# Loading one-hots of places from a table, splitting the queries into three bf16 parts, and gathering 110 of 220 pairs of tiles without an add

## The chip, the cores and the metric

The kernel runs on one core of a Trainium2 chip. The time is the device time of the whole kernel in microseconds (us). Before the change three runs gave 3959.79, 3951.86 and 3950.71 us, a median of 3951.86 us.

## The reference, cut to what matters

Four graph layers run one after the other on 3,125 nodes with 256 channels and 53,125 edges, sorted by destination. Each adds its result to the node rows and normalizes them. The fourth, which the change is mostly about, is a transformer convolution that runs twice (here called its two halves):

```python
q = (x @ Wq + bq).reshape(n, H, C)          # H = 4 heads, C = 64 channels
k = (x @ Wk + bk).reshape(n, H, C)
v = (x @ Wv + bv).reshape(n, H, C)
e = (edge_attr @ We + be).reshape(-1, H, C)
k_j = k[src] + e
q_i = q[dst]
alpha = jnp.einsum('ehc,ehc->eh', q_i, k_j) / jnp.sqrt(C)
...                                          # softmax of alpha over the edges of each dst
msg = (v[src] + e) * alpha[..., None]
out = jax.ops.segment_sum(msg, dst, num_segments=n)
```

The first layer and the third are attention layers too, with one score for a node in place of a row of queries: an edge needs the score of its destination.

## The kernel before

**Tiles.** The edges are cut into 440 tiles of 128 (`ET`), each of which has its destinations in one block of 128 nodes (25 blocks, `NT`). Two tiles are a pair (220 pairs), eight tiles a group (`HB`, 55 groups), sixteen tiles a batch of the softmax (`NB`). The program is a row of phases with a barrier between them: `start_up`, `aggregate0`, `finish0`, `aggregate1`, `finish1`, `aggregate2`, `finish2`, `attend(1)`, `between`, `attend(2)`, `last_rows`. `finish2` and `between` make queries, keys and values of the fourth layer from the node rows (class `Projection`), and `attend` goes over the edges.

**One-hots of places.** TensorE fetches the destination's row for each edge by a matmul with a one-hot matrix `ohT` (places in the block by edges). `lo_tab` in DRAM holds each edge's place as bf16. For each group the SyncE queue (SP) spreads 1,024 places over 128 partitions (`lo_b`, 256 KB), and VectorE (DVE) compares them with the partition's number: `places(g)` in `aggregate2` (line 1348) and `attend` (line 1761), `one_hots(g)` in `aggregate0` (line 532). In `attend` the one-hots and the queries `H` are f32; in the aggregates one-hots and scores are bf16, the scores as three bf16 parts that are summed.

**attend, a step for each pair p.** Each engine has its order written out, and semaphores join them:

- GpSimd (POOL) issues an indirect DMA for each tile that gathers 128 rows of `kv_tab` (keys, values, and four columns for weights: 516 f32) by source. In 55 of the 220 pairs (`plain(p)`, p % 8 in (4, 6)) the rows are written to the buffer `kv` (line 1737). In the others the DMA adds them to what stands there (`compute_op=ALU.add`, line 1741), which are the edge terms.
- TensorE (PE) makes the edge terms of a pair (`edge_terms`, line 1922), f32, six steps ahead for a pair with an add and one step ahead for a plain pair, then the queries of pair p + 1 (`queries`, line 1933), then the scatter of pair p - 11 (`scatter`, line 1951).
- ScalarE (ACT) copies the edge terms from PSUM to `kv` twice, as key and as value part, for pairs with an add (`fill(p + 5)`, lines 1862 and 1863), makes the one-hots of the scatter, and weighs two of four heads.
- DVE, for a plain pair, adds the edge terms to keys and values (`add_edge_terms`, lines 1769 and 1771). For each pair it multiplies keys by queries (`times_q`, line 1781), sums by channels (line 1787), adds two windows of sums to `acc` (line 1817), and takes its share of the softmax. Once in four pairs it makes a group's one-hots of places (line 1761) and weighs two heads (line 1795).
- SP loads for each group the edge attributes (`aT`, 512 KB, line 1748) and the places (line 1751), each when a ring of three has room.

**finish2 and between.** For each of 25 blocks t, PE turns the rows (`turn`), ACT copies them (`take_turned`, line 1521), PE multiplies them by the weights (`products`, line 1513), and DVE takes the four results with their biases (`take`, lines 1538 to 1544), the queries into `H`. The rows are turned two blocks ahead.

## Time and profile before

| | before |
|---|---|
| median of three runs | 3951.86 us |
| profiled execution, its own time | 3946.54 us |
| its span, first to last instruction | 3944.8 us |
| busy: PE, DVE, POOL, ACT | 2936.7, 2698.3, 2560.9, 1981.6 us |
| mean granted TensorE clock | 0.869 of full speed |
| stretch of aggregate2 / finish2 / attend(1) | 587 / 139 / 803 us |
| stretch of between / attend(2) | 112 / 801 us |

Busy times are unions of an engine's instructions, which overlap a little. PE's are modelled at their ends. The stretches are cut at phase ends read from the timeline, and their sum of five is 2442 us of the span.

### The profile page before, as it was taken

To read this page: it belongs to the slowest core of one execution; us is meant where nothing else is said; L and a number is where in the kernel's file an instruction comes from. 1 tells how busy PE (TensorE), PEld (TensorE's weight loads), DVE (VectorE), ACT (ScalarE), POOL (GpSimd) and SP (SyncE) were. 2 spreads that over 40 slices of the span, in tenths; PEclk is the share of its full clock that TensorE was granted. 3 is DMA by queue.
4 is the path that set the end of the run, shared out by engine and by line. 5 is a ranking of instruction groups with operands and counts; after the bars stand their busy time and mean duration, and the time that the engine had idled before them with its cause. 6 is when DMAs were issued, how large, how long until landed. Compare 5 with 4: busy or idle time off the path is not lost. (4 is left out here: it accounts for less than half of the span.)

```text
span 3944.8 us, 52281 instructions
## 1 busy us (share of the span) xinstructions
PE 2936.7 (74%) x11541; PEld 2078.5 (53%) x11541; DVE 2698.3 (68%) x6381; ACT 1981.6 (50%) x5915; POOL 2560.9 (65%) x2236
## 2 busy tenths in 40 slices
PE   5666774677776946777749788888887788888884
PEld 4444443444444624555534566666663466666762
DVE  4556567555553645666666588888886588898887
ACT  3444454111111433333333488887882288888885
POOL 4777773677775017777730688888870488888881
PEclk7777776889998977778779899999998899999997
DMA  4644443777777224444433899999993799999994
GB/s 142 141 130 119 132 133 91 220 232 227 231 230 188 67 69 133 133 132 131 131 65 119 197 210 209 212 204 212 206 184 119 191 208 212 209 210 212 209 208 100
DMA packets 370541, 661.49 MB, mean 168 GB/s; under 512 B 64401, under 2 KB 166785, under 8 KB 370242
## 3 DMA queue, kind: packets, MB, share of 16 engines
q0 software_dynamic: 176384, 406.78, 48.6%
q1 hardware_dynamic: 189746, 247.54, 20.0%
q10 hardware_dynamic: 4112, 3.83, 0.3%
q8 instruction: 110, 1.80, 0.2%
q14 instruction: 189, 1.55, 0.1%
HBM read 582.61 MB, written 75.32 MB: 167 GB/s over the span
## 5 line engine op out<-in xcount | busy, mean ns | idle before, releaser
L1741 POOL DMA_INDIRECT t_kv<-kv_tab,srcT x664 | 1041.4, 1568 | 327.2 <-issue 194.5
L1951 PE MATMUL bank<-t_kv,t_oh 128*128 128x260 f32 x1760 | 488.3, 401 | 93.7 <-ACT t_oh L1874 84.6
L1330 POOL DMA_INDIRECT grow<-h_tab,srcT x440 | 416.8, 947 | 198.4 <-issue 88.3
L487 POOL DMA_INDIRECT grow<-h_tab,srcT x440 | 430.8, 979 | 164.0 <-issue 94.4
L797 POOL DMA_INDIRECT grow<-x_tab,srcT x440 | 417.0, 948 | 153.6 <-issue 95.4
L1922 PE MATMUL bank<-we,t_aT 128*128 128x256 f32 x1760 | 465.3, 399 | 19.2 <-DMA t_aT<-attrT_tab 17.1
L1933 PE MATMUL bank<-H,t_ohT 128*128 x1760 | 465.3, 388 | 16.8 <-DVE t_ks L1781 16.4
L1905 ACT ACTIVATE t_kv<-t_kv 128x64 f32<-128x64 f32 x1760 | 461.6, 333 | 0.0
L1781 DVE TENSOR_TENSOR t_ks<-t_kv,bank 128x512 f32<-128x512 f32 x440 | 300.4, 683 | 192.5 <-DMA t_kv<-kv_tab,srcT 173.8
L1951 PEld LDWEIGHTS bank<-t_kv,t_oh 128*128 128x128 f32 x1760 | 307.8, 193 | 183.9 <-ACT t_oh L1874 114.7
L932 PE MATMUL bank<-grow,oh 128*128 128x272 f32 x880 | 300.1, 451 | 139.2 <-DMA grow<-x_tab,srcT 88.7
L1922 PEld LDWEIGHTS bank<-we,t_aT 128*128 128x128 f32 x1760 | 339.4, 198 | 80.1 <-DMA t_aT<-attrT_tab 18.7
L1817 DVE TENSOR_TENSOR acc<-acc,bank 128x260 f32 x880 | 365.9, 416 | 21.4 <-PE bank L1951 15.5
L845 DVE TENSOR_TENSOR acc<-acc,bank 128x272 f32 x440 | 192.4, 437 | 274.8 <-PE bank L932 239.6
L644 PE MATMUL bank<-grow,oh 128*128 128x258 f32 x880 | 332.6, 545 | 57.3 <-DVE acc L557 49.5
L1933 PEld LDWEIGHTS bank<-H,t_ohT 128*128 128x128 f32 x1760 | 338.3, 196 | 68.8 <-issue 22.5
L1455 PE MATMUL bank<-grow,oh 128*128 128x257 f32 x880 | 315.9, 495 | 17.2 <-DVE acc L1378 10.2
L880 ACT COPY aT<-bank 128x512 f32<-128x512 f32 x110 | 64.4, 585 | 486.2 <-PE bank L905 478.5
L1872 ACT ACTIVATE t_oh<-iota_n,dlocT 128x128 f32<-128x128 f32 x880 | 302.9, 393 | 0.0
L644 PEld LDWEIGHTS bank<-grow,oh 128*128 128x128 f32 x880 | 229.4, 276 | 137.0 <-ACT grow L619 80.4
L932 PEld LDWEIGHTS bank<-grow,oh 128*128 128x128 f32 x880 | 154.0, 205 | 236.2 <-DMA grow<-x_tab,srcT 160.5
L557 DVE TENSOR_TENSOR acc<-acc,bank 128x258 f32 x440 | 186.7, 424 | 124.6 <-DVE acc L557 56.4
(382 smaller groups left out, 5145.4 us busy)
## 6 DMA issues: line engine op xcount, KB each, us to landing
t_aT<-attrT_tab SPq DMA_DIRECT2D x110, 512.0 KB, 8.5
lob<-lo_tab SPq DMA_DIRECT2D x110, 256.0 KB
arow<-in_edge_attr SPq DMA_DIRECT2D x440, 64.0 KB
attrT_tab<-aT SPq DMA_DIRECT2D x55, 512.0 KB
t_lob<-lo_tab SPq DMA_DIRECT2D x110, 256.0 KB
grow<-h_tab,srcT POOLq DMA_INDIRECT x880, 2.8
t_kv<-kv_tab,srcT POOLq DMA_INDIRECT x880, 6.7
kv_tab<-kv SPq DMA_DIRECT2D x8, 1290.0 KB, 5.2
```

What stands on the lines that cost most here:

```text
L487: nc.gpsimd.indirect_dma_start(out=grow[:, t % RA, :], out_offset=None, in_=h_tab, in_offset=bass.IndirectOffsetOnAxis(ap=srcT[:, t:t + 1] ...
L644: nc.tensor.matmul(PS[t % WIN][:, 0:F + 2], oh[:, g % 2, u, :], grow[:, t % RA, :], start=True, stop=True).then_inc(products, 1)
L797: nc.gpsimd.indirect_dma_start(out=grow[:, t % RA, 0:F], out_offset=None, in_=x_tab, in_offset=bass.IndirectOffsetOnAxis(ap=srcT[:, t:t + ...
L932: nc.tensor.matmul(PS[t % WIN1][:, 0:AC], oh[:, g % 2, u, :], grow[:, t % RA, :], start=True, stop=True).then_inc(products, 1)
L1330: nc.gpsimd.indirect_dma_start(out=grow[:, t % R2, :], out_offset=None, in_=h2_tab, in_offset=bass.IndirectOffsetOnAxis(ap=srcT[:, t:t + 1 ...
L1455: nc.tensor.matmul(PS[2 + t % WIN2][:, 0:F + 1], oh[:, t // HB % 2, t % HB, :], grow[:, t % R2, 0:F + 1], start=True, stop=True).then_inc( ...
L1741: nc.gpsimd.indirect_dma_start(out=kv[:, u, :], out_offset=None, in_=kv_tab, in_offset=row, compute_op=ALU.add).then_inc(g_ready[u], 16)
L1817: nc.vector.tensor_tensor(window, window, PS[4 + t % WIN3][:, 0:LHW], ALU.add).then_inc(added, 1)
L1905: last = nc.scalar.activation(part, part, ACT.Copy, scale=u_rows[:, t % UB, h, C3:C3 + 1])
L1922: mm = nc.tensor.matmul(PS[j % 2][:, v * F:(v + 1) * F], aT[:, g % 3, u * P:(u + 1) * P], we[:, :], start=True, stop=True)
L1933: mm = nc.tensor.matmul(PS[2 + p % 2][:, v * F:(v + 1) * F], ohT[:, g % 2, u * P:(u + 1) * P], H[:, ds(blocks[u], 1), :].rearrange("p b f ...
L1951: nc.tensor.matmul(PS[4 + t % WIN3][:, 0:LHW], oh[:, t // HB % 2, t % HB, :], kv[:, t % UB, F:KVW], start=True, stop=True).then_inc(produc ...
```

## The change

Three things change together.

1. `aggregate0` writes the one-hots that it makes, bf16, to a new table in DRAM, `place_tab` (256 KB a group, 55 groups). `aggregate2` and `attend` load them from there in place of the places, with a ring of three, and the compares of DVE (lines 1348 and 1761) are gone.
2. The queries are kept as three bf16 parts whose sum is the f32 value (`Q3`, in a buffer `room` that `H` is a view of). In `finish2` and `between` DVE writes the query rows to a ring `q` of ten. ACT casts them to the high part, POOL subtracts it, ACT casts the middle part, POOL subtracts it, ACT casts the low part. In `attend` a tile's queries are three bf16 matmuls that add up in PSUM, in place of one f32 matmul.
3. `plain(p)` is now p % 2 == 1: 110 pairs of 220 are gathered plainly. The ring of the scatter's one-hots in `attend` shrinks from 16 tiles to ten.

Some buffers of earlier phases move into `room` to make space. The core of the diff:

```diff
@@ aggregate0, SyncE
-                        for g in range(NH):
+                        for g in range(NH + 4):
                             if g >= 4:
                                 sp.wait_ge(oht_ready, g - 3)
-                            sp.dma_start(lo_b[:, g % 4, :], lo_tab[...]).then_inc(lo_in[g % 4], 16)
+                                sp.dma_start(place_tab[g - 4, :, :], ohT[:, (g - 4) % 3, :]).then_inc(oht_out[(g - 4) % 3], 16)
+                            if g < NH:
+                                sp.dma_start(lo_b[:, g % 4, :], lo_tab[...]).then_inc(lo_in[g % 4], 16)
@@ aggregate0, VectorE
-                            if g >= 2:
-                                dve.wait_ge(z_terms, g - 1)
-                            nc.vector.tensor_scalar(ohT[:, g % 2, :], lo_b[:, g % 4, :], iota_p[:, 0:1], None, ALU.is_equal).then_inc(oht_ready, 1)
+                            if g >= 3:
+                                dve.wait_ge(z_terms, g - 2)
+                                dve.wait_ge(oht_out[g % 3], g // 3 * 16)
+                            nc.vector.tensor_scalar(ohT[:, g % 3, :], lo_b[:, g % 4, :], iota_p[:, 0:1], None, ALU.is_equal).then_inc(oht_ready, 1)
@@ class Projection
+            def round_queries(self, act, t):
+                if t < NT:
+                    act.wait_ge(self.mm_taken, 2 * t + 1)
+                    nc.scalar.copy(Q3[:, t, 0, :], self.q[:, t % (2 * GRP), :]).then_inc(self.hi_ready, 1)
+                if 0 <= t - 1 < NT:
+                    act.wait_ge(self.rest1_ready, t)
+                    nc.scalar.copy(Q3[:, t - 1, 1, :], self.rest[:, (t - 1) % 4, :]).then_inc(self.mid_ready, 1)
+                if 0 <= t - 2 < NT:
+                    act.wait_ge(self.rest2_ready, t - 1)
+                    nc.scalar.copy(Q3[:, t - 2, 2, :], self.rest[:, (t - 2) % 4, :]).then_inc(self.low_ready, 1)
+
+            def query_rests(self, pool, t):
...
+                    nc.gpsimd.tensor_tensor(self.rest[:, t % 4, :], self.q[:, t % (2 * GRP), :], Q3[:, t, 0, :], ALU.subtract).then_inc(self.rest1_ready, 1)
...
+                    nc.gpsimd.tensor_tensor(self.rest[:, (t - 1) % 4, :], self.rest[:, (t - 1) % 4, :], Q3[:, t - 1, 1, :], ALU.subtract).then_inc(self.rest2_ready, 1)
@@ take, VectorE
-                nc.vector.scalar_tensor_tensor(H[:, t, :], qk[:, 0:F], 0.125, b_all[:, 0:F], ALU.mult, ALU.add)
+                if t >= 2 * GRP:
+                    dve.wait_ge(self.rest1_ready, t - 2 * GRP + 1)
+                nc.vector.scalar_tensor_tensor(self.q[:, t % (2 * GRP), :], qk[:, 0:F], 0.125, b_all[:, 0:F], ALU.mult, ALU.add)
@@ finish2, ScalarE, at the end of step i
                             copies(i - 2, 3, GRP)
+                            for t in range((i - 3) * GRP, (i - 2) * GRP):
+                                if t >= 0:
+                                    pr.round_queries(act, t)
+                        for t in range((NG - 1) * GRP, NT + 2):
+                            pr.round_queries(act, t)
@@ attend
-            return p % 8 in (4, 6)
+            return p % 2 == 1
@@ attend, SyncE
                             if g >= 3:
-                                sp.wait_ge(oht_ready, g - 2)
-                            sp.dma_start(lo_b[:, g % 3, :], lo_tab[...]).then_inc(lo_in[g % 3], 16)
+                                sp.wait_ge(q_ready, 4 * (g - 2))
+                            sp.dma_start(ohT[:, g % 3, :], place_tab[g, :, :]).then_inc(oht_in[g % 3], 16)
@@ attend, VectorE
-                            if p % 4 == 1 and (p + 3) // 4 < NH:
-                                places((p + 3) // 4)
@@ attend, TensorE, queries
-                                mm = nc.tensor.matmul(PS[2 + p % 2][:, v * F:(v + 1) * F], ohT[:, g % 2, u * P:(u + 1) * P],
-                                                      H[:, ds(blocks[u], 1), :].rearrange("p b f -> p (b f)"), start=True, stop=True)
+                                for n in range(3):
+                                    mm = nc.tensor.matmul(PS[2 + p % 2][:, v * F:(v + 1) * F], ohT[:, g % 3, u * P:(u + 1) * P],
+                                                          Q3[:, ds(blocks[u], 1), n, :].rearrange("p b f -> p (b f)"), start=(n == 0), stop=(n == 2))
@@ between, ScalarE
-                        for t in range(NT):
-                            pr.take_turned(act, t)
+                        for t in range(NT + 6):
+                            if t < NT:
+                                pr.take_turned(act, t)
+                            if t >= 4:
+                                pr.round_queries(act, t - 4)
```

What VectorE has in a row in the middle of `attend(1)`, from one plain pair on. Before (line 1769 and 1771 add edge terms, 1781 multiplies by queries, 1817 adds a window, 1787 sums by channels, 1761 makes one-hots of places):

```order
L1769 TENSOR_TENSOR t_kv<-t_kv,bank 128x2x256
L1771 TENSOR_TENSOR t_kv<-t_kv,bank 128x2x4x64
L1781 TENSOR_TENSOR t_ks<-t_kv,bank 128x512
...
L1817 TENSOR_TENSOR acc<-acc,bank 128x260
L1787 TENSOR_REDUCE t1s_al<-t_ks 128x2x4
...
L1781 TENSOR_TENSOR t_ks<-t_kv,bank 128x512
...
L1787 TENSOR_REDUCE t1s_al<-t_ks 128x2x4
...
L1761 TENSOR_SCALAR t_ohT<-t_lob,iota_p 128x1024
L1769 TENSOR_TENSOR t_kv<-t_kv,bank 128x2x256
```

And with the change, where these lines are 1801, 1803, 1813, 1849 and 1819:

```order
L1801 TENSOR_TENSOR t_kv<-t_kv,bank 128x2x256
L1803 TENSOR_TENSOR t_kv<-t_kv,bank 128x2x4x64
L1813 TENSOR_TENSOR t_ks<-t_kv,bank 128x512
...
L1849 TENSOR_TENSOR acc<-acc,bank 128x260
L1819 TENSOR_REDUCE t1s_al<-t_ks 128x2x4
...
L1813 TENSOR_TENSOR t_ks<-t_kv,bank 128x512
...
L1819 TENSOR_REDUCE t1s_al<-t_ks 128x2x4
...
L1801 TENSOR_TENSOR t_kv<-t_kv,bank 128x2x256
```

The compare is gone, and the two additions come with every second pair.

What TensorE has in a row in `attend(1)` around the queries of a pair. Before (an ISA row sets the matmul's address from a register):

```order
L1951 MATMUL bank5<-t1_kv,t1_oh 128x260
L1922 MATMUL bank1<-we,t1_aT 128x256 x2
L1922 MATMUL bank0<-we,t1_aT 128x256 x2
L146 TENSOR_LOAD block_i
L1933 ISA
L1933 MATMUL bank2<-H,t1_ohT 128x256
L1933 ISA
L1933 MATMUL bank2<-H,t1_ohT 128x256
L1951 MATMUL bank6<-t1_kv,t1_oh 128x260
```

With the change the same place reads (lines 1981, 1951 and 1963 are the scatter, the edge terms and the queries; the two rows of 1963 stand six times, of which two are shown):

```order
L1981 MATMUL bank5<-t1_kv,t1_oh 128x260
L150 TENSOR_LOAD block_i
L1963 ISA
L1963 MATMUL bank2<-H,t1_ohT 128x256
L1963 ISA
L1963 MATMUL bank2<-H,t1_ohT 128x256
...
L1981 MATMUL bank6<-t1_kv,t1_oh 128x260
...
L1951 MATMUL bank1<-we,t1_aT 128x256 x2
L1951 MATMUL bank0<-we,t1_aT 128x256 x2
```

Two f32 matmuls with two address settings became six bf16 ones with six, and both edge terms stand in every second step.

What ScalarE has in a row near the end of `finish2`. Before, it is only copies of turned rows (`x11`: the last eleven), and the phase is over:

```order
L1653 ACT_TABLE_LOAD
L1653 ACTIVATE small<-small 128x5
L1521 COPY xT<-bank 128x256
L1658 ACTIVATE X<-hc,small 128x256 x5
L1521 COPY xT<-bank 128x256 x11
```

With the change, five blocks' casts (lines 1530, 1533 and 1536, three a block) stand between runs of copies (line 1525), and twelve steps of casts come behind the last copies:

```order
L1691 ACTIVATE X<-hc,small 128x256 x5
L1525 COPY xT<-bank 128x256 x3
L1530 CAST H<-q 128x256
L1533 CAST H<-rest 128x256
L1536 CAST H<-rest 128x256
...
L1525 COPY xT<-bank 128x256 x5
...
L1525 COPY xT<-bank 128x256 x3
L1530 CAST H<-q 128x256
```

A cast that waits for POOL holds the copies behind it, and with them PE's next products.

## Rows read from the trace of the kernel before

**Rows 1.** Stretches by phase: busy (instructions) of each engine, clock, DMA share, GB/s.

```profile
core 0: us, PE busy (x) PEld busy (x) DVE busy (x) ACT busy (x) POOL busy (x), PEclk, DMA share, GB/s
1456.00:2043.00 587.00, 411.94 (x1572) 276.97 (x1572) 368.30 (x1086) 188.95 (x497) 416.77 (x440) 0.77 0.47 124
2043.00:2182.00 139.00, 95.11 (x250) 43.67 (x250) 82.00 (x284) 48.79 (x126) 6.24 (x5) 0.83 0.33 113
2182.00:2985.00 803.00, 668.97 (x2892) 523.83 (x2892) 674.21 (x1462) 629.16 (x1956) 632.74 (x440) 0.96 0.95 199
2985.00:3097.00 112.00, 94.95 (x250) 43.44 (x250) 66.63 (x154) 9.31 (x25) 6.16 (x5) 0.92 0.49 164
3097.00:3898.00 801.00, 669.65 (x2892) 525.60 (x2892) 674.57 (x1467) 627.84 (x1955) 627.79 (x440) 0.96 0.95 200
```

**Rows 2.** The middle of attend(1), same columns.

```profile
2250.00:2900.00 650.00, 549.32 (x2433) 435.74 (x2432) 565.80 (x1235) 526.78 (x1645) 536.09 (x374) 0.98 0.99 209
```

**Rows 3.** Waits in that stretch: total us, times, longest us.

```profile
POOL t_kv L1741 <- issue: 83.2, 273, 0.3
DVE t_ks L1781 <- DMA t_kv<-kv_tab,srcT: 63.2, 40, 4.1
```

**Rows 4.** POOL by line, whole span: busy us, mean ns, idle before.

```profile
L1741 POOL DMA_INDIRECT t_kv<-kv_tab,srcT x664 | 1041.4, 1568 | 327.2 <-issue 194.5 <-ACT t_kv L1863 132.8
L1737 POOL DMA_INDIRECT t_kv<-kv_tab,srcT x216 | 219.1, 1014 | 65.8 <-issue 65.2 <-PE bank L1951 0.6
L1566 POOL MEMSET acc<- 128x1360 f32 x5 | 6.2, 1247 | 80.7 <-DVE hc L1580 80.7
```

**Rows 5.** First and last start (us) of the sums by channels, both halves.

```profile
L1787 DVE TENSOR_REDUCE t1s_al<-t_ks x220: 662/680/689, 2196.8 to 2957.2; 128x8 f32<-128x512 f32 x110
L1787 DVE TENSOR_REDUCE t2s_al<-t_ks x220: 662/680/690, 3115.7 to 3870.9; 128x8 f32<-128x512 f32 x110
```

**Rows 6.** DVE by line, 2250 to 2900 us.

```profile
L1781 DVE TENSOR_TENSOR t_ks<-t_kv,bank 128x512 f32<-128x512 f32 x186 | 126.9, 682 | 73.7 <-DMA t_kv<-kv_tab,srcT 63.2 <-PE bank L1933 10.1 <-issue 0.3
L1761 DVE TENSOR_SCALAR t_ohT<-t_lob,iota_p 128x1024 f32<-128x1024 bf16 x46 | 38.5, 836 | 0.0
L1771 DVE TENSOR_TENSOR t_kv<-t_kv,bank 128x512 f32<-128x512 f32 x46 | 31.2, 679 | 0.0
L1769 DVE TENSOR_TENSOR t_kv<-t_kv,bank 128x512 f32<-128x512 f32 x46 | 31.1, 676 | 0.8 <-PE bank L1922 0.8
```

**Rows 7.** DVE in order of time: start us, us.

```profile
2514.24 0.68 DVE L1769 TENSOR_TENSOR t_kv<-t_kv,bank 128x512 f32<-128x512 f32 x1
2515.43 0.68 DVE L1781 TENSOR_TENSOR t_ks<-t_kv,bank 128x512 f32<-128x512 f32 x1
```

**Rows 8.** DMA queues, 2250 to 2900 us: packets, MB, share of 16 engines.

```profile
q0 software_dynamic: 47892, 98.69, 80.9%
q1 hardware_dynamic: 13461, 36.65, 18.0%
```

**Rows 9.** The same for aggregate2, 1456 to 2043 us.

```profile
q0 software_dynamic: 21120, 58.15, 38.8%
```

**Rows 10.** Edge attributes (line 1748), 2250 to 2900 us, issue to landing.

```profile
DMA to landing us min/median/max: 6.1/9.1/12.5
```

**Rows 11.** ACT by line, 2250 to 2900 us.

```profile
L1863 ACT COPY t_kv<-bank 128x512 f32<-128x512 f32 x139 | 80.2, 577 | 0.0
```

**Rows 12.** PE by line in that stretch, and register steps of line 1436 (whole span).

```profile
L1933 PE MATMUL bank<-H,t_ohT 128*128 x741 | 192.8, 383 | 0.0
L1436 PEldq FUSED_REGOPS  x440: 46/46/46, 1459.7 to 2007.4; - x147
```

**Rows 13.** End of finish2 in order of time, PE, ACT and SP.

```profile
2166.14 7.03 PE L1513 MATMUL bank<-wq,xT 128*128 128x512 f32 x16
2166.34 0.37 ACT L1521 COPY xT<-bank 128x256 f32<-128x256 f32 x1 [3.28 <-PE bank L1502]
2178.11 0.34 SPq L1748 DMA_DIRECT2D t_aT<-attrT_tab  x1
```

More of the change, by code:

```diff
@@ L465, in aggregate0 @@
             lo_in = (lo_in0, lo_in1, lo_in2, lo_in3)
+            oht_out = [sem(f"a0_oht_out{u}") for u in range(3)]
             ends_in, d_in, c_ready, c_out, c_in, f_ready, f_out, f_in = [sem("seg_" + n) for n in "ends_in d_in c_ready c_out c_in f_ready f_out f_in".split()]
             R, per = H3 * NB, NBT * P // 2
-            Hf = H[:, :, :].rearrange("p t f -> p (t f)")
+            Hf = room_flat
             dB = Hf[:, 0:per].bitcast(BF16).rearrange("p (b e) -> p b e", b=NBT)
@@ L1383, in _ @@
                         step(copied)
-                        places(0)
                         one_hots(0)
@@ L1397, in _ @@
                                 g = 2 * b + j // 4
-                                if j % 4 == 1 and g + 1 < NH:
-                                    places(g + 1)
                                 gc = 2 * c + j // 4
@@ L1552, in finish2 @@
         def finish2():
+            early.close()
             h_ready, n_ready, t_ask, t_ready, var_ready, std_ready, f_ready, x_ready, x_out, dv, ac = [
@@ L1566, in _ @@
                             nc.gpsimd.memset(group(acc, i), 0.0).then_inc(acc_zero, 1)
+                            for t in range((i - 1) * GRP, i * GRP):
+                                if t >= 0:
+                                    pr.query_rests(pool, t)
+                        for t in range((NG - 1) * GRP, NT + 1):
+                            pr.query_rests(pool, t)
                     @block.vector
@@ L1821, in _ @@
                         dve.wait_ge(zeroed, 2)
-                        places(0)
                         blocks = following = None
@@ L1998, in _ @@
                             nc.gpsimd.memset(group(acc, i), 0.0).then_inc(acc_zero, 1)
+                            for t in range((i - 1) * GRP, i * GRP):
+                                if t >= 0:
+                                    pr.query_rests(pool, t)
+                        for t in range((NG - 1) * GRP, NT + 1):
+                            pr.query_rests(pool, t)
                     @block.sync
```

113 lines of the change are left out of this document (59 added, 54 removed).

## The prediction

> **What bounds the kernel now.** I read the busy time by phase first [rows 1]. The two halves of the fourth layer take 803 and 801 of 3945 us, and there four engines are busy for 78 to 84% of the time and the DMA engines for 95%. No other phase has its engines that full, and nearly all that changes lies in these two. So I took a stretch from the middle of the first half, 2250 to 2900 us [rows 2], and asked who waits there.
>
> POOL does not wait for anyone. Its gathers follow one another with a gap of 83.2 / 273 = 0.305 us that is put down to its own issue [rows 3], and its 374 gathers fill the stretch: 536.1 + 374 x 0.305 = 650 of 650 us [rows 2]. Its pace can also be built from its two kinds of gather [rows 4]. One with an add takes 1.568 us and a plain one 1.014 us, each with 0.305 us behind it. Eight pairs of today's pattern are 12 adds and 4 plain ones, 12 x 1.873 + 4 x 1.319 = 27.75 us, or 3.47 us a pair. The real pace, from the first and the last sum by channels over 219 steps, is (2957.2 - 2196.8) / 219 = 3.47 us in the first half and (3870.9 - 3115.7) / 219 = 3.45 in the second [rows 5]. I use 3.46. So POOL sets the pace, and DVE waits for gathers, 63.2 us of the stretch, 0.34 us a pair (186 pairs) [rows 3, 6].
>
> Two others stand close behind. The DMA engines' share is 0.99 [rows 2], 80.9% for gathers and 18.0% for SP's loads [rows 8]. DVE is busy for 565.8 / 186 = 3.04 us a pair and idle for 0.45, of which 0.34 is the wait for gathers and 0.11 is everything else [rows 2, 3]. Shortening POOL's work is worth only what these two leave.
>
> **Plain pairs, 110 in place of 55.** POOL: eight pairs become 8 adds and 8 plain gathers, 8 x 1.873 + 8 x 1.319 = 25.5 us, 3.19 us a pair (it was 3.47) [rows 4]. DMA: the trace has no view that parts adds from plain gathers, so I take the plain one from aggregate2, whose 440 gathers move half the bytes each: 0.388 x 587 / 440 = 0.52 us of all engines, doubled 1.04 us [rows 9]. The add is then (0.809 x 650 - 94 x 1.04) / 280 = 1.53 us, with a quarter of the 374 gathers plain, so 94 and 280. SP's loads are 0.180 x 650 / 186 = 0.63 us a pair, and keep their bytes [rows 8]. A pair now costs 2 x (1.53 + 1.04) / 2 + 0.63 = 3.20 us of DMA, where it was 3.44. DVE: each further plain pair has the two additions of 31.1 and 31.2 us for 46 pairs [rows 6]. Neighbours overlap a little: two of 0.68 us take 1.19 us from start to start, 0.085 less for each [rows 7]. A quarter of the pairs gets them anew, 62.3 / 186 - 0.5 x 0.085 = +0.29 us a pair. ACT loses two copies of some 0.57 us in a quarter of the pairs [rows 11], about 0.28 us; it isn't a bound (526.8 / 186 = 2.83 us a pair [rows 2]).
>
> **Loaded one-hots.** DVE loses the compare, 38.5 us for 46 groups [rows 6], 0.207 - 0.25 x 0.085 = -0.19 us a pair. The load that takes the place of the load of places has the same 256 KB, so DMA is as before. It now waits for the queries of the group three back, and is needed nine steps later, some 29 us; SP's loads of edge attributes land within 12.5 us [rows 10]. I cost that at nothing. In aggregate2 the same edit takes work from DVE, but there POOL fills 416.8 + 440 x 0.305 = 551 of 587 us [rows 1], so 0, with -5 as the other end. In aggregate0 the 55 stores are 14.4 MB. By queue q1's 36.65 MB in 18.0% of 650 us [rows 8], they are 46 us of DMA time, spread over a phase that gathers as often as aggregate2, and DVE asks for a slot's store only three groups (some 30 us) after it is made: +1 us, 0 to +5.
>
> **DVE's new pace.** 3.04 - 0.19 + 0.29 = 3.15 us busy, and with today's other idle time of 0.11 it is 3.26. It passes POOL (3.19) and DMA (3.20) and becomes the bound. All three lie within 2%, so I add 0.02 for waits that hit each other and take **3.28 us a pair**: (3.28 - 3.46) x 438 = **-79 us** for both halves. The ends: POOL's 3.19 gives -118; 3.40, a third of today's wait for gathers left on top of DVE's 3.28, gives -26.
>
> **Three bf16 parts in attend.** Today a pair's four matmul records take 192.8 / 741 x 4 = 1.04 us of PE [rows 12]. There will be six matmuls, each with a register step of 46 ns on the weight queue, as line 1436 has it [rows 12]. A bf16 matmul of 256 columns has no row. Above it can't cost more than an f32 record, 0.26 us; below I take half of that, 0.13, since the f32 matmul of the same columns takes two records. It is nearest to the lower end, as its operands have half the bytes and the register step fits beneath. Six are 0.78 us (at the upper end 1.56), and PE goes from 549.3 / 186 = 2.95 to 2.69 us a pair, below the pace. It hides behind DVE. At the upper end PE has 3.47 and the cover is gone; that is a rival below.
>
> **Rounding the queries.** In finish2 and between, 25 blocks each have three casts on ACT and two subtractions on POOL. A cast is like ACT's copy of 256 columns, 0.37 us [rows 13], so 1.1 us a block. POOL's subtraction has no row. Below it: a memset of 1,360 columns takes 1.247 us [rows 4], for 256 columns 0.23. Above: its plain gather's 1.01 us [rows 4]. I take 0.6, since two operands are read and one written where DVE needs 0.68 us for 512 columns [rows 7]. A block then takes 2 x 0.6 and a little waiting, 1.3 us, and POOL leads. The Trainium skill (GPSIMD Engine Reference, section on elementwise cycle accounting) gives 4497 ns for an add of 2,048 f32 columns; an estimate from that is 0.56 us for 256, and the sum would be the same within 1 us. No row here shows it.
>
> PE paces these phases with 3.65 us a block: ACT idles 3.28 us beside a copy of 0.37 [rows 13]. In between, ACT's 1.1 us and POOL's 1.2 fit there block by block: +1 us, 0 to +5. In finish2, ACT casts five blocks at a time between its copies. That is 6.5 us in which it takes no turned row, and PE, two blocks ahead, has some 5 us of cover; four such places cost +3 us. Behind its last copy at 2166.3 + 0.4 there are twelve steps, 15.6 us, so it ends at 2182.3, where today the next phase starts at 2178.1 [rows 13]: +4. Together **+7 us**, from 0 (subtractions of 0.3 us, twelve steps of 1.1) to +20 (subtractions of 1.0).
>
> **The sum.** -79 + 7 + 1 + 1 = -70 us. Against the profiled execution's own 3946.5 us that is 3876; the median of the three runs stands 5 us higher (3951.9), and gives 3882. I say **3879 us**.
>
> **Rivals.**
>
> 1. *POOL stays the bound.* DVE's 0.11 us of other idle time may be hidden once it is always late, and then DVE has 3.15, below POOL. The pace is 3.19, and the time 3951.9 - 118 + 9 = 3843 us. For it: much of that idle time is the wait for queries, 10.1 us [rows 6], which PE's lighter work shortens. Against: DVE would need to be fed without a gap at 99% of the pace.
> 2. *The edge attributes come late.* A plain pair's edge terms are made one step ahead, so now the last ones of each group are, and the next load into that slot goes out four steps (13.1 us) before it is needed; today it is five steps (17.3 us) in every second group and ten in the others. The landing takes 9.1 us in the median and 12.5 at most [rows 10]. PE has the queries queued behind that wait, and DVE waits for those. One wait of 1 us in half of 110 groups is +55 us, and the time is 3934. Against: DMA has less to do than now.
> 3. *PE becomes the bound*, the slower side. If a bf16 matmul with an address from a register costs as much as an f32 record, 0.26 us, PE has 3.47 us of work a pair, and with 0.1 for waits the pace is 3.57: +0.11 x 438 + 9 = +57, 4009 us. It decides from 0.24 us a matmul. Against: the register step itself is 46 ns.
> 4. *TensorE's clock falls.* It is at 0.98 in the stretch with PE busy for 85% [rows 2], and at 0.77, nearly half of the time at 1.2 GHz, in aggregate2 with PE busy for 70% [rows 1]. After the change PE is busy for 2.69 / 3.28 = 82%. If the clock fell to aggregate2's, PE's 2.69 us would grow by 0.46 of it to 3.9, and the time by some 200 us to 4150. The Trainium skill says the same of the array (TensorE: Matmul & The Clock Gate, What's actually happening): activity releases the throttle, and idle time brings it back. By that rule less work on PE speaks against this edit. Against: 82% is much nearer to 85 than to 70.
> 5. *The change does not do what it says for the pace*: waits eat the gain of POOL wholly. DVE's busy time rises, so its slack of 0.45 us must carry everything; at 3.44 and more the time is within 0.3% of before.
>
> **Chances.** My forecast's pace of 3.22 to 3.36: 0.68. Rival 1: 0.13. Rival 2 or a part of 5 that leaves some gain: 0.09. No change: 0.03. Rival 3: 0.05, rival 4: 0.02. A measurement can tell 0.3%, 12 us, from no change. Faster by more: 0.68 + 0.13 + 0.07 = 0.88; within it 0.05; slower 0.07. The range goes from POOL's bound to a pace of 3.37 with a finish2 at its upper end (3951.9 - 40 + 15): 3838 to 3925.
>
> **What would show the steps.** POOL's gathers should have gaps beyond 0.3 us behind waits for ACT's fills, where it has none now; DVE's share in the middle should be 96% (now 87%), its wait for gathers under 0.1 us a pair; the steps between sums by channels 3.28 us; queries on PE 0.78 us a pair, six records; the DMA share near 0.97; ACT's casts behind the last copy of finish2, and the next phase some 7 us later. I am wrong if DVE still waits for gathers at a pace above 3.35 (then DMA or the lead of five pairs is the bound), if PE waits for edge attributes, or if the clock in the middle is below 0.9.

## The result, and the profile after

The changed kernel takes 3929.69 us in the median of five runs (3925.82 to 3934.51), the kernel before 3950.99 us (3949.83 to 3959.79). The ratio is 0.9939, interval 0.9924 to 0.9953: faster by some 21 to 24 us, 0.6%. I had said 3879 us, from 3838 to 3925. The sign is right, but some 70% of the forecast gain did not come, and the time is 5 us above the range.

First the stretches by phase of the changed kernel, with the columns of [rows 1], and the middle of the first half:

```profile
1456.00:2042.00 586.00, 415.14 (x1572) 279.98 (x1572) 344.86 (x1026) 187.67 (x496) 415.88 (x440) 0.77 0.47 125
2042.00:2181.00 139.00, 94.55 (x250) 43.33 (x250) 80.54 (x279) 72.47 (x198) 35.96 (x53) 0.86 0.31 108
2181.00:2976.00 795.00, 651.43 (x3332) 484.75 (x3332) 697.80 (x1524) 583.75 (x1848) 567.22 (x443) 0.95 0.89 202
2976.00:3088.00 112.00, 94.12 (x250) 43.15 (x250) 71.79 (x154) 33.59 (x100) 42.89 (x55) 0.94 0.49 164
3088.00:3881.00 793.00, 648.72 (x3332) 483.35 (x3332) 697.68 (x1524) 581.20 (x1843) 567.61 (x440) 0.95 0.88 202
2250.00:2900.00 650.00, 546.45 (x2883) 410.87 (x2882) 598.68 (x1311) 502.16 (x1595) 494.20 (x384) 0.97 0.94 216
```

aggregate2 is as long as before (586 us), with DVE 23 us less busy for nothing, as POOL fills that phase. The middle stretch now has 190 pairs where 186 were [rows 2]. DVE's share rose from 87 to 92%, and not to the 96% that I had forecast. The DMA share fell to 0.94, POOL is no longer full, and the clock is 0.97. So nothing is full: the kernel waits on itself. The starts of the sums by channels give the pace (first and last start, as in [rows 5]):

```profile
L1819 DVE TENSOR_REDUCE t1s_al<-t_ks x220: 662/683/695, 2199.5 to 2948.9; 128x8 f32<-128x512 f32 x110
L1819 DVE TENSOR_REDUCE t2s_al<-t_ks x220: 660/683/692, 3104.2 to 3853.6; 128x8 f32<-128x512 f32 x110
```

749.4 / 219 = 3.422 us a pair in both halves, where 3.28 was forecast and 3.47 and 3.45 were measured before. The halves are 11.0 and 5.8 us shorter. The two spans differ by 17.6 us: these 16.8, another 3.2 between the halves (158.5 us from the last sum of one to the first of the next, now 155.3), 0.3 at the end, and 2.7 us given back ahead of the first sum.

The waits of the same stretch, as in [rows 3], say where DVE's time goes:

```profile
ACT t_kv L1891 <- PE bank L1951: 51.2, 49, 1.4
...
POOL t_kv L1779 <- ACT t_kv L1892: 47.7, 29, 3.0
...
DVE t1s_fm L1314 <- PE bank L1271: 22.7, 24, 1.9
DVE t1s_tiles L1285 <- PE bank L1261: 19.1, 24, 0.8
```

In this stretch DVE has no wait for gathers left, where it had 63.2 us [rows 3]. It waits for PE, in two places, each once in every batch of eight pairs (24 batches): 22.7 + 19.1 = 41.8 us, 0.22 us a pair. Both are answers within the running softmax: line 1261 turns the run of maxima (the softmax's part 1), line 1271 spreads the factors (part 5). Before the change the list of the same stretch has only this of the two (lines 1303 and 1260 are the later 1314 and 1271), and none for the other:

```profile
DVE t1s_fm L1303 <- PE bank L1260: 2.0, 4, 0.6
```

DVE is busy for 598.7 / 190 = 3.15 us a pair, which is what I had summed up, and idle for 0.27, where I had put 0.11. ACT waits for edge terms (line 1951) before it can fill, and POOL for the fills. That came as foretold, and in this stretch it makes DVE wait for no gather.

Here is one of the two waits in order of time (start us, us, engine, line; PE and DVE lines of one even step):

```profile
2525.74 0.39 PE L1258 MATMUL bank<-t1s_flip,t1s_al 128*128 128x128 f32 x2
...
2525.97 1.89 PE L1951 MATMUL bank<-we,t_aT 128*128 128x256 f32 x8
2526.20 0.42 DVE L1281 TENSOR_TENSOR_SCAN t1s_run<-pen_next,bank 128x128 f32<-128x128 bf16 x1
...
2527.69 0.82 PE L1963 MATMUL bank<-H,t_ohT 128*128 x6
...
2528.35 0.27 PE L1261 MATMUL bank<-ident,t1s_run 128*1 128x128 f32 x1
...
2528.66 0.29 DVE L1285 TENSOR_TENSOR_SCAN t1s_tiles<-pen_tile,bank 1x71 f32<-1x71 bf16 x1 [0.80 <-PE bank L1261]
```

DVE's scan is done at 2526.6. Its answer on PE stands behind eight records of edge terms, 1.89 us, and six of queries. Eight records are **two** pairs of edge terms. The diff doesn't show this, but two lines of PE's loop together do: edge terms of a pair with add are made six pairs ahead (AHEAD + 1), those of a plain pair one ahead. With plain pairs at p % 2 == 1, both p + 6 with an add and p + 1 plain fall on even p. So each even step has two pairs of edge terms ahead of its queries and of the softmax's part of that step that DVE waits for, and each odd step none. The softmax has its three steps at p % 8 = 0, 1 and 2, two of them even. The old pattern gave the steps p % 8 = 0 to 7 none, one, one, two, one, two, none and one pair. So step 0, with the answer of line 1261, went from none to two, and step 2, with that of line 1271, from one to two.

### The profile page after: what moved, and what is told of

Read it like the earlier page. It is cut to its first block and busy times, and to the rows that moved or that the text cites. A ratio compares the mean times of both kernels' runs of the same rounds, so it can differ in the third digit from the quotient of the medians.

```text
span 3927.2 us, 55865 instructions
## 1 busy us (share of the span) xinstructions
PE 2893.9 (74%) x12421; PEld 1996.5 (51%) x12421; DVE 2729.7 (70%) x6440; ACT 1937.5 (49%) x5841; POOL 2498.7 (64%) x2336
## 5 line engine op out<-in xcount | busy, mean ns | idle before, releaser
L1779 POOL DMA_INDIRECT t_kv<-kv_tab,srcT x440 | 692.8, 1575 | 232.9 <-ACT t_kv L1892 118.0
L1981 PE MATMUL bank<-t_kv,t_oh 128*128 128x260 f32 x1760 | 532.1, 415 | 145.7 <-DVE acc L1849 103.0
L1340 POOL DMA_INDIRECT grow<-h_tab,srcT x440 | 416.6, 947 | 197.6 <-issue 95.0
L493 POOL DMA_INDIRECT grow<-h_tab,srcT x440 | 428.8, 975 | 164.7 <-issue 97.5
L1775 POOL DMA_INDIRECT t_kv<-kv_tab,srcT x440 | 440.4, 1001 | 134.1 <-issue 129.0
L1951 PE MATMUL bank<-we,t_aT 128*128 128x256 f32 x1760 | 453.8, 404 | 21.1 <-DMA t_aT<-attrT_tab 21.1
L1981 PEld LDWEIGHTS bank<-t_kv,t_oh 128*128 128x128 f32 x1760 | 292.6, 197 | 260.2 <-issue 122.9
L1951 PEld LDWEIGHTS bank<-we,t_aT 128*128 128x128 f32 x1760 | 357.5, 207 | 79.6 <-DMA t_aT<-attrT_tab 22.7
L1963 PE MATMUL bank<-H,t_ohT 128*128 x2640 | 372.8, 276 | 21.1 <-DVE t_ks L1813 16.5
L655 PE MATMUL bank<-grow,oh 128*128 128x258 f32 x880 | 324.0, 534 | 73.6 <-DVE acc L568 61.2
L1963 PEld LDWEIGHTS bank<-H,t_ohT 128*128 128x128 bf16 x2640 | 257.8, 98 | 120.0 <-issue 38.2
L891 ACT COPY H<-bank 128x512 f32<-128x512 f32 x110 | 64.4, 585 | 484.6 <-PE bank L916 484.6
L655 PEld LDWEIGHTS bank<-grow,oh 128*128 128x128 f32 x880 | 226.8, 270 | 146.3 <-ACT grow L630 90.4
```

Of the source, the lines that this page charges most:

```text
L493: nc.gpsimd.indirect_dma_start(out=grow[:, t % RA, :], out_offset=None, in_=h_tab, in_offset=bass.IndirectOffsetOnAxis(ap=srcT[:, t:t + 1] ...
L655: nc.tensor.matmul(PS[t % WIN][:, 0:F + 2], oh[:, g % 2, u, :], grow[:, t % RA, :], start=True, stop=True).then_inc(products, 1)
L1340: nc.gpsimd.indirect_dma_start(out=grow[:, t % R2, :], out_offset=None, in_=h2_tab, in_offset=bass.IndirectOffsetOnAxis(ap=srcT[:, t:t + 1 ...
L1775: nc.gpsimd.indirect_dma_start(out=kv[:, u, :], out_offset=None, in_=kv_tab, in_offset=row).then_inc(g_ready[u], 16)
L1779: nc.gpsimd.indirect_dma_start(out=kv[:, u, :], out_offset=None, in_=kv_tab, in_offset=row, compute_op=ALU.add).then_inc(g_ready[u], 16)
L1951: mm = nc.tensor.matmul(PS[j % 2][:, v * F:(v + 1) * F], aT[:, g % 3, u * P:(u + 1) * P], we[:, :], start=True, stop=True)
```

## The experiments

Theory A: DVE's new idle time is this doubling. Each kernel is timed against the kernel before in its own group of runs, so ratios are compared and not times. The groups are e1 to e4, e5 to e8 and e9 to e12. The changed kernel itself was run for the result above and in the second group (e5). In the other two the kernel before takes 300 us more, and the changed kernel has no time there. The pace is worked out as above, from the first and the last sum by channels.

**e1: the other parity.** The doubled edge terms fall on odd steps, of which the softmax uses one.

```diff
-            return p % 2 == 1
+            return p % 2 == 0 and p > 0
```

> The changed kernel with the plain pairs on the even numbers but 0 (109 of 220). PE then makes both edge terms of a step in odd steps. Theory A (PE's order: two pairs of edge terms, 1.9 us, stand ahead of the transposes and sums of the softmax that DVE waits for, in the first and third step of each batch, which are even): only the middle step of a batch has both, so one of the two waits goes and a smaller one may come; the pace falls from 3.42 to about 3.33 us a pair, 3890 us. Theory B (DVE, once it is the bound, loses 0.27 us a pair to handoffs wherever they stand): 3.42, 3930 us. Theory C (the lead of POOL, ACT and PE over DVE is too short for the new order, so gathers' fills come late): 3.42, 3930 us.

Ratio 0.9778, interval 0.9762 to 0.9794; (3209.5 - 2499.6) / 219 = 3.24 us a pair, 3.26 in the second half. This is better than A had asked for, with the same instructions but for one plain pair fewer. From 2550 to 3150 us DVE has no wait for lines 1261 and 1271 left. In the middle step the doubled edge terms stand ahead of line 1267, and DVE's wait for that is small:

```profile
DVE t1s_d L1305 <- PE bank L1267: 8.4, 5, 1.7
```

Theory B, idle time wherever the handoffs stand, falls with this run.

**e4 and e8: an even lead.** With four or six pairs of lead, edge terms of either kind alternate, one pair in each step.

```diff
-        AHEAD = 5
+        AHEAD = 4
```

(In e8 the new line is `AHEAD = 6`.)

> The changed kernel with the lead of POOL's adds at four pairs in place of five. PE's edge terms then part evenly, one pair in each step. Theory A: one pair (1.0 us) ahead of the chain in place of two, DVE's waits for PE go, the pace falls to about 3.25 us, 3855 us. Theory B: 3.42, 3930 us. Theory C: the lead is shorter, so DVE waits for gathers again; slower than 3.42, 3950 us or more.

> A lead of six pairs where there are five. Theory A (it is the parity: with an odd lead and plain odd pairs, every even step makes two pairs of edge terms ahead of the sums that DVE waits for; with an even lead each step makes one): 3.24 us a pair, as with a lead of four. Rival C (a shorter lead helps by itself, since fills and gathers stand less in each other's way): slower than the lead of five, above 3.42 us a pair. Rival D (a longer lead is better for gathers): as A or a little below it, 3.20.

A lead of four: ratio 0.9750 (0.9733 to 0.9768), pace (3203.9 - 2495.6) / 219 = 3.23. A lead of six: ratio 0.9736 (0.9722 to 0.9749), and its sums are

```profile
L1819 DVE TENSOR_REDUCE t1s_al<-t_ks x220: 661/679/689, 2198.0 to 2903.1; 128x8 f32<-128x512 f32 x110
L1819 DVE TENSOR_REDUCE t2s_al<-t_ks x220: 661/679/689, 3057.9 to 3766.4; 128x8 f32<-128x512 f32 x110
```

3.22 and 3.24 us a pair. Shorter and longer than five are alike, so the length of the lead is not what counts (theories B and C and rivals C and D fall); whether it is odd is. Of DVE's waits for lines 1261 and 1271 one of 1.0 us is left in the middle of e8 (2250 to 2900 us), and none in e4 (2550 to 3200).

**e5: the changed kernel again**, in the group of e6 to e8.

> The changed kernel itself, on the same chip as the others of this group, to be the measure for them. Both theories: the same ratio to the kernel before as it had, 0.994, within 0.003, and 3.42 us a pair in both halves.

Ratio 0.9941 (0.9927 to 0.9955), 3.41 us a pair: as expected.

**e6: the other parts alone**, the one-hots and the bf16 queries with the old pattern of plain pairs.

```diff
-            return p % 2 == 1
+            return p % 8 in (4, 6)
```

> The other parts of the change alone: one-hots loaded, queries in three bf16 parts, but plain pairs 4 and 6 of eight, as before. Theory A (POOL sets the pace of the old pattern, whatever the others do): pace 3.46 us a pair as before, finish2 6 us longer, so 7 us more than before, ratio 1.002. Rival B (the loaded one-hots or the bf16 queries themselves bring the gain or the loss): a pace that differs from 3.46 by more than 0.03 us, that is by more than 13 us.

Ratio 1.0023 (1.0014 to 1.0033), 9 us slower; (2961.8 - 2199.3) / 219 = 3.48 us a pair. The middle of its first half, with the columns of [rows 2]:

```profile
2250.00:2850.00 600.00, 501.57 (x2602) 381.14 (x2601) 494.66 (x1101) 488.58 (x1525) 494.81 (x346) 0.94 1.00 210
```

POOL and DMA are as full as before, DVE is at 82% where it was at 87. So with the old pattern these parts give DVE free time that nobody uses. Theory A holds within its 0.03 us, rival B does not. The span is 10.3 us longer than before. finish2 is 7.5 us longer (as in the changed kernel, below), but the halves are slower too, by 2.1 and 6.6 us, in which POOL's gathers take 5.4 us more in all. The rest, 5.9 us less, is start, handover and end. Why the gathers took longer no run tells.

**e3: edge terms behind the scatter.** If PE makes the edge terms six ahead last in its step, nothing of the doubling stands ahead of the softmax.

```diff
...
-                            if p + AHEAD + 1 < PAIRS and not plain(p + AHEAD + 1):
-                                edge_terms(p + AHEAD + 1)
...
                             if 0 <= q < PAIRS:
                                 scatter(q)
+                            if p + AHEAD + 1 < PAIRS and not plain(p + AHEAD + 1):
+                                edge_terms(p + AHEAD + 1)
```

> The changed kernel with one edit in PE's order in both halves: the edge terms that are made six steps ahead stand behind the scatter of their step, not ahead of the queries. Nothing else moves. Theory A: the waits of DVE for the transpose and the sum of the softmax shrink by the 1 us that no longer stands ahead of them, so to about none; the pace falls to about 3.25 us, 3855 us. Theory B: 3.42, 3930 us. Theory C: the fills come later still, so 3.42 or slower.

The lines left out ahead of it swap the same two kinds in `edge_order`, which says which pair takes which bank; so "nothing else moves" leaves this out. It is the same in e9.

A plain miss of theory A: ratio 1.0618 (1.0601 to 1.0636), 4.08 us a pair. Theory C had the direction (fills later still, 3.42 or slower), and no size. The waits from 2700 to 3150 us:

```profile
ACT t_kv L1891 <- PE bank L1951: 152.8, 55, 4.3
POOL t_kv L1779 <- ACT t_kv L1892: 106.4, 51, 3.6
PE bank L1981 <- ACT t_oh L1903: 60.1, 35, 2.3
PE bank L1981 <- ACT t_kv L1934: 41.6, 18, 2.3
```

By these waits it is a ring: the scatter (1981) waits for ACT's one-hots and weighing (1903, 1934), the edge terms (1951) are queued behind the scatter, ACT's fill (1891) waits for them, and the next one-hots and weighing are queued behind the fill. PE's and ACT's parts of a step no longer overlap. I had not looked at who is queued behind the fill.

**e9: edge terms behind the softmax's second part, ahead of the scatter.** Made to tell the ring from the doubling.

```diff
...
-                            if p + AHEAD + 1 < PAIRS and not plain(p + AHEAD + 1):
-                                edge_terms(p + AHEAD + 1)
...
                             if batch:
                                 sm.pe(pe, batch[0], 2 * batch[1] + 1, sums_done, 0)
+                            if p + AHEAD + 1 < PAIRS and not plain(p + AHEAD + 1):
+                                edge_terms(p + AHEAD + 1)
                             if 0 <= q < PAIRS:
```

> A lead of five, as in the changed kernel, but on PE the edge terms of the pair six ahead stand behind the queries and the second softmax part of the step, and ahead of its scatter (in e3 they stood behind the scatter). Theory A (DVE waits for the second softmax part because two pairs of edge terms are ahead of it): one pair, 0.95 us, is left ahead, DVE's waits of 0.8 and 0.9 us all but go, and the pace falls to 3.23 to 3.28 us. Theory A's reading of e3 (there the ring was scatter, edge terms, ACT's fill, ACT's weighing, scatter) says that this place has no ring. Rival G (any later place of these edge terms makes ACT's fills late, and they set the pace): above 3.42 us.

Ratio 0.9891 (0.9877 to 0.9905), 3.37 us a pair: faster than the changed kernel by some 20 us, but a quarter to a third of the doubling's price and not all of it. The two waits went as A says (from 2620 to 3120 us, line 1261 is left with 0.4 us and line 1271 with none), and a third took their place, in all 18 batches; the list has three of them behind line 1258 and names none for the others:

```profile
DVE t1s_run L1281 <- issue: 16.8, 15, 1.1
DVE t1s_run L1281 <- PE bank L1258: 3.2, 3, 1.1
```

One of them in order of time:

```profile
2723.74 1.11 PE L1981 MATMUL bank<-t_kv,t_oh 128*128 128x260 f32 x4 [1.43 <-DVE acc L1849]
2724.69 0.38 PE L1257 MATMUL bank<-ident,t1s_al 128*128 128x128 f32 x2
...
2725.34 0.42 DVE L1281 TENSOR_TENSOR_SCAN t1s_run<-pen_next,bank 128x128 f32<-128x128 bf16 x1 [1.12 <-issue]
```

The scatter of step 7 is now late, and the softmax's first part (1257, 1258) stands behind it; DVE's scan starts when line 1258 is through. ACT is late ahead of that scatter: its fill had waited 1.10 us for the edge terms, and its weighing, which the scatter needs, came behind the fill:

```profile
2720.82 0.58 ACT L1891 COPY t_kv<-bank 128x512 f32<-128x512 f32 x1 [1.10 <-PE bank L1951]
...
2722.92 1.05 ACT L1934 ACTIVATE t_kv<-t_kv 128x64 f32<-128x64 f32 x4
```

From 2620 to 3120 us ACT waits 77.5 us ahead of its fills (line 1891). So without the scatter ahead of the edge terms the pace of 4.08 is gone, as the ring says, and rival G (above 3.42) falls by its number. A's size for this kernel (3.23 to 3.28) was wrong, and ACT's late fills, which G names, are in the wait that is left. How much of it they make up isn't parted.

**e2: plain pairs in a block.** Pairs 4 to 7 of eight; two pairs of edge terms fall only on steps 3 to 5, away from the softmax.

```diff
-            return p % 2 == 1
+            return p % 8 in (4, 5, 6, 7)
```

> The changed kernel with the same number of plain pairs, 110, but the last four of each eight, p % 8 in (4, 5, 6, 7). PE's two steps with part of the softmax's chain that DVE waited for have none or one pair of edge terms. Theory A: DVE's waits for PE fall from 1.75 us a batch to under 0.4, the pace to 3.21 to 3.26 us a pair, 3835 to 3860 us. Theory B: 3.42, 3930 us. Theory C: four adds in a row on POOL (15 us) against the lead of five pairs make it worse, 3.45 or more, 3940 us or more.

Ratio 1.0062 (1.0039 to 1.0084), (3271.3 - 2502.2) / 219 = 3.51 us a pair: slower than before, where A had said 3.21 to 3.26. C's number came (3.45 or more), but not its mechanism, as DVE doesn't wait for gathers from 2650 to 3150 us. DVE's waits for lines 1261 and 1271 are gone there too, so A's reading of the changed kernel is not contradicted, but something else takes more. Of DVE's 49.6 us of idle time in that stretch 37.0 stand ahead of its window additions, which by the code wait for PE's scatter (the DMA that the first row names belongs to a phase long past):

```profile
DVE acc L1849 <- DMA place_tab<-H: 22.6, 14, 2.5
DVE acc L1849 <- PE bank L1981: 7.7, 8, 2.2
DVE acc L1849 <- issue: 6.7, 4, 2.5
```

The scatter stands behind the edge terms in PE's queue. What the edge terms (line 1951, weight loads and matmuls together) waited for, over the whole span (us, times):

```profile
  DVE t_kv L1803: 51.5, 77
  DMA t_aT<-attrT_tab: 44.4, 4
  ACT t_kv L1892: 32.8, 63
```

In the changed kernel the first of these is 1.4 us, in e1, e4 and e8 10.7, 16.8 and 12.2, and the last is 0.5 or less. Edge terms have two banks, so the j-th pair of them in PE's order waits until the pair two places ahead of it has been used. Where kinds alternate, that is an older pair. In a block it is pair p while PE makes the terms of p + 1: PE's step waits for DVE's addition (line 1803) of that same step, with the queries and the scatter queued behind it. That this makes the pace is argued and not shown: from 2650 to 3150 us the matmuls of line 1951 wait only 4.0 us for DVE's additions and 3.8 us for ACT's fills, and DVE has no wait for queries. A third bank wasn't tried, and what holds the scatter back stays open. The DMA engines, too, run unevenly: between 121 and 306 GB/s in the slices from 2650 to 3150 us, in e1 between 188 and 238.

**e7: the best mix.** A lead of four, and the casts of finish2 spread between its copies.

```diff
                                 pr.take_turned(act, t)
+                                if t >= 4:
+                                    pr.round_queries(act, t - 4)
...
-                            for t in range((i - 3) * GRP, (i - 2) * GRP):
-                                if t >= 0:
-                                    pr.round_queries(act, t)
-                        for t in range((NG - 1) * GRP, NT + 2):
+                        for t in range(NT - 4, NT + 2):
```

> A lead of four pairs, and in finish2 ACT rounds a block of queries behind each turned row it copies, four blocks back, so that six steps stand behind its last copy where there are twelve. Theory A: 3.24 us a pair, as with the lead of four alone, so some 80 us less than the changed kernel of this group; and finish2 ends 6 us earlier than in the changed kernel (six steps of 1.26 us fewer, less a little that PE now waits for turned rows). If ACT's casts between the copies hold PE up, finish2 is as long as in the changed kernel or longer.

3841.29 us, ratio 0.9709 (0.9695 to 0.9724), against 3930.4 of the changed kernel in this group: 89 us less, the fastest here. The pace is 3.23. SP's first load of the next phase goes out at 2183.14 us, in e8 at 2182.68, but that doesn't mean that the spreading won nothing, for in e7's execution finish2 also starts 5.7 us later. Below, e8 first, the first start of ACT's squares marks the start of finish2, and the first start of SP's load its end:

```profile
L1672 ACT ACTIVATE sq<-hc x25: 398/400/417, 2043.5 to 2091.5; 128x256 f32<-128x256 f32 x25
L1786 SPq DMA_DIRECT2D t_aT<-attrT_tab x110: 332/333/580, 2182.7 to 3721.9; - x110
L1674 ACT ACTIVATE sq<-hc x25: 399/401/419, 2049.2 to 2097.9; 128x256 f32<-128x256 f32 x25
L1785 SPq DMA_DIRECT2D t_aT<-attrT_tab x110: 332/333/652, 2183.1 to 3723.9; - x110
```

So finish2 takes 139.2 us in e8 and 133.9 in e7. By the same two rows all kernels with the casts in blocks have 139.2 to 140.8, and all with spread casts (e7, e10, e11, e12) 133.9 to 134.7: the spreading saves 5 to 6 us, as expected. Of the 89 us some 81 are the halves.

What bounds e7? Its gathers from 2250 to 2850 us, with the columns of [rows 4]:

```profile
L1778 POOL DMA_INDIRECT t_kv<-kv_tab,srcT x187 | 300.0, 1604 | 57.0 <-issue 57.0
L1774 POOL DMA_INDIRECT t_kv<-kv_tab,srcT x188 | 186.1, 990 | 57.3 <-issue 43.3 <-PE bank L1980 14.0
```

300.0 + 57.0 + 186.1 + 57.3 = 600.4 of 600 us: POOL is full again, DVE is at 97.5%, the DMA engines at 0.97. Three kernels ask which of them it is.

**e10: half of an addition left out.** Half of the keys of plain pairs stay without their edge terms, which spares DVE some 0.17 us a pair.

```diff
-            nc.vector.tensor_tensor(kv[:, s:s + 2, 0:F], kv[:, s:s + 2, 0:F], e, ALU.add).then_inc(k_added, 1)
+            nc.vector.tensor_tensor(kv[:, s:s + 2, 0:F // 2], kv[:, s:s + 2, 0:F // 2], e[:, :, 0:F // 2], ALU.add).then_inc(k_added, 1)
```

> As e7, but DVE's addition of the edge terms to the keys of a plain pair (one of its two) takes half of the columns, so that the other half of the keys stays without them: 0.17 us less of DVE work a pair. If POOL is the bound of e7 (its gathers and the issue behind them fill 600 of 600 us there): no change, 3.22 us a pair within 0.01, 0.971 of before. If DVE is: at least 0.05 less, some 25 us or more below e7.

Ratio 0.9761 (0.9748 to 0.9774), pace 3.25 and 3.27: no gain, rather a little loss. e7 was not run in this group; e4, with the same lead in a group whose kernel before is as slow (4251 us, here 4266), had 0.9750 and 3.23. DVE is free earlier, and waits for gathers instead, from 2620 to 3120 us:

```profile
DVE t_ks L1812 <- DMA t_kv<-kv_tab,srcT: 17.7, 13, 2.5
```

**e11 and e12: three and five plain pairs of eight** on top of e7.

```diff
-            return p % 2 == 1
+            return p % 8 in (1, 3, 5)
```

```diff
-            return p % 2 == 1
+            return p % 8 in (1, 3, 4, 5, 7)
```

> As e7, with 3 plain pairs of eight (1, 3 and 5) in place of 4. By e7's own gathers, 1.91 us for one with an add and 1.30 us for a plain one with the issue behind them, POOL needs (10 x 1.91 + 6 x 1.30) / 8 = 3.36 us a pair, and DVE 3.0: pace 3.32 to 3.36, some 40 to 60 us above e7. If DVE were the bound of e7, it would be no slower than e7.

> As e7, with 5 plain pairs of eight (1, 3, 4, 5 and 7). POOL needs (6 x 1.91 + 10 x 1.30) / 8 = 3.06 us a pair, DVE 3.15 + 0.15 = 3.30: pace 3.30 to 3.35, some 35 to 55 us above e7, and DVE is the bound, with POOL waiting for slots or fills. If POOL alone counted, 3.1 and faster.

Three: ratio 0.9914 (0.9901 to 0.9926), 3.42 and 3.41 us a pair, a little above the range expected. Five: 1.0039 (1.0025 to 1.0052), 3.54 and 3.56, far above it. With three, POOL is full (500.3 of the 500 us from 2620 to 3120), DVE waits for gathers again (42.1 us), and the plain gathers are longer than the sum had them (1.08 us, 0.99 in e7):

```profile
L1778 POOL DMA_INDIRECT t_kv<-kv_tab,srcT x182 | 292.4, 1607 | 55.5 <-issue 55.5
L1774 POOL DMA_INDIRECT t_kv<-kv_tab,srcT x110 | 118.9, 1080 | 33.5 <-issue 31.1 <-PE bank L1980 2.4
```

With five it isn't DVE's busy time (93% of the same stretch) that costs, as I had said, but waits again:

```profile
POOL t_kv L1778 <- ACT t_kv L1891: 82.6, 29, 4.8
...
DVE t1s_tiles L1285 <- DMA gates<-gh_tab: 24.4, 13, 2.0
```

Line 1285 waits for the turned maxima of line 1261; the load that its row names ended long before. With its other rows line 1285 has 29.6 of DVE's 36.3 us of idle time, although only one pair of edge terms stands ahead of line 1261 here. So two pairs are not the only thing that makes this answer late. It looks like e2's case: pairs 3, 4 and 5 are plain in a row, and PE's edge terms (line 1950 here) wait for DVE's addition for 87.6 us of the span, where e7 has 15.4. That these waits are the cause isn't shown.

```profile
  DVE t_kv L1802: 87.6, 108
```

## Why the prediction was wrong, point by point

- **What bounds the kernel before: right.** With the old pattern the pace stays near POOL's (3.48, before 3.47 and 3.45) when DVE and PE are relieved (e6).
- **DVE's new busy time: right.** 3.15 us a pair forecast, 3.15 measured.
- **"With today's other idle time of 0.11 it is 3.26": this step failed.** It took idle time for a property of DVE. Half of it (10.1 of 21 us [rows 6]) was an answer from PE, the queries, and such answers depend on what PE's queue holds ahead of them. In the changed kernel that wait is gone, but the idle time is 0.27 us a pair, 0.22 of it behind two pairs of edge terms in even steps. By the spans the steps of the two halves took 1498.8 us, where 3.28 x 438 = 1436.6 were forecast: 62 us more. Some 10 us less than forecast lie elsewhere: 5 us ahead of the first sum, 4 between the halves, 0.3 at the end. That leaves 52 us by the spans, and 51 against the 3879 us. With the lead even, the same work runs at 3.22 to 3.24 (e4, e7, e8), where DVE's other idle time is again below 0.11 us a pair and the forecast's sum holds, with a little to spare.
- **How it could have been seen.** The traces and the loop of before show each piece: 0.26 us for an f32 record, four records a pair, no edge terms in step 0 and one pair in step 2. What lacked was to write PE's queue out for p % 8 = 0, 1 and 2. I looked at that order for the load of edge attributes (rival 2) and not for the softmax's answers behind the same instructions.
- **Edge attributes late (rival 2): not seen.** They land in 5.9 us in the median, [rows 10] had 9.1, and PE doesn't wait for them.
- **PE's queries: right.** 159.8 us for 190 pairs is 0.84 us a pair, six records of 0.14 us (forecast 0.78, before 1.04 [rows 12]):

```profile
L1963 PE MATMUL bank<-H,t_ohT 128*128 x1146 | 159.8, 274 | 2.2 <-issue 0.9
```

  PE as a whole has 2.88 us a pair where I had 2.69. The queries are 0.06 of the difference and the scatter's busy time 0.11 (227.1 / 190 = 1.20, before 202.4 / 186 = 1.09), whose reason no run tells. Rival 3 was far off. Of rival 4, the granted clock stayed at 0.97, nearly always 2.4 GHz, with PE busy for 84% of the stretch. In e6, with about the same share, it was 0.94, and in e7, with 86%, 1.00.
- **finish2: right in mechanism and size.** From ACT's first square to SP's first load of the next phase it takes 139.2 us in the changed kernel (2045.0 to 2184.2) and 140.7 in e5, before 131.7 (2046.4 to 2178.1): +7.5 and +9, forecast +7. (The load's own time, 2184.2 against 2178.1 [rows 13], shows +6, but the start of the phase moves by up to 7 us from one execution to another, 2042.5 in e6 and 2049.3 in e5.) Behind the start of PE's last products there are 15.8 us where 12.0 were, +3.8 (forecast +4). The steps behind ACT's last copy take 1.26 us (forecast 1.3), in the changed kernel:

```profile
2173.51 0.40 ACT L1530 CAST H<-q 128x256 bf16<-128x256 f32 x1
...
2174.46 0.41 ACT L1536 CAST H<-rest 128x256 bf16<-128x256 f32 x1 [0.23 <-POOL rest L1546]
2174.77 0.40 ACT L1530 CAST H<-q 128x256 bf16<-128x256 f32 x1
```

  A subtraction on POOL takes 0.66 us (forecast 0.6), 0.63 from one start to the next:

```profile
2170.62 0.66 POOL L1543 TENSOR_TENSOR rest<-q,H 128x256 f32<-128x256 f32 x1
2171.25 0.66 POOL L1546 TENSOR_TENSOR rest<-rest,H 128x256 f32<-128x256 f32 x1
```

  The Trainium skill's figure, by which I had estimated 0.56 us (GPSIMD Engine Reference, section on elementwise cycle accounting), is further off than mine, and the measurement decides. 3.4 us of finish2's loss came back: the first sum of the first half starts 15.3 us after that phase's first load, where it was 18.7. That was not in my sum. The loaded one-hots of the first group are at most a third of it: e6 has them with the old pattern, and there it is 17.6 us. The rest comes with the pattern of plain pairs.
- **Rival 5, "waits eat the gain", was the case that came**, in the part that leaves some gain (3.422, where its bound for none was 3.44), and I had given that and rival 2 together a chance of 0.09. It had no mechanism; with one it would have had a price and a larger chance. (The upper end of the range, 3925, was 2 us below its own sum, 3951.9 - 40 + 15 = 3927, which changes nothing.) **Rival 1, POOL stays the bound at 3.19**, is what the kernels with an even lead come near to.

## What to carry to other kernels

When a change alters which steps of a loop have an instruction, write out one whole period of each in-order queue, before and after, and look at who is waited for behind it; two rules that depend on p through different offsets (p + 1 and p + 6) can meet in the same step. Idle time of an engine is not a constant that goes along into the next sum: ask for each part of it whose answer it is, and what stands ahead of that answer. Moving work to the end of a queue is safe only when nobody's queue holds, behind the wait for it, something that this queue waits for; where that isn't so, look for a shift that parts the two rules. Here it was a lead of 4 or 6 in place of 5, worth some 80 us, with no instruction added.

## What the runs showed of the hardware

- **A gather's time on POOL is not only POOL's work.** The plain gather takes 0.99 us in e7, 1.00 in the changed kernel, 1.08 in e11 and 1.15 in e9, at the same shape and bytes, so it seems to hold some wait that no view parts from work. Whether POOL or the DMA engines (share 0.97) bound e7 is therefore open; e10 speaks against DVE, as less work for it brought no gain.
- **The same kernel takes 300 us more in some groups of runs, and by phase.** The kernel before takes 3951 us with the result and 3955 with e5 to e8, but 4251 with e1 to e4 and 4266 with e9 to e12. e5 to e8 and e9 to e12 ran on the same chip (number 3), so it isn't the chip alone. The halves run alike in both (3.23 us a pair in e4 and in e7); the difference lies ahead of them. In aggregate2, the first addition to `acc` is 541.8 us ahead of the last in the changed kernel, and 615.5 in e4, whose POOL gathers take the same 0.946 us each but stand idle longer (197.6 us in the changed kernel):

```profile
L1340 POOL DMA_INDIRECT grow<-h_tab,srcT x440 | 416.4, 946 | 289.2 <-issue 103.7 <-POOLq L84 68.1 <-PE bank L1456 67.0
```

  Why, no run here tells.
- **A bf16 matmul of 256 columns with an address from a register** takes 0.14 us in a row of six, where an f32 record took 0.26 [rows 12]; so three bf16 parts in place of f32 save 0.2 us a pair.
